# Two staging buffers for the pieces of G, and the final normalization on GpSimd

## What is computed

```python
queries = (query @ Wq + bq).reshape(B, L, H, E)
keys_flat = k @ Wk + bk                      # k: the 32 patterns, the same for every batch
values = (keys_flat @ Wv + bv).reshape(B, S, H, D)
A = sparsemax(einsum('blhe,bshe->bhls', queries, keys) / sqrt(E))
out = einsum('bhls,bshd->blhd', A, values)
x = layernorm(x + transpose(out, (0, 2, 1, 3)).reshape(B, L, H * D) @ Wo + bo)
s = einsum('btd,dm->btm', x, Win) + bin_
g = einsum('btmh,mh->btm', relu(s[..., None] * W1 + b1), W2) + b2
x = layernorm(x + einsum('btm,md->btd', g, Wout) + bout)
```

## Time and profile before

| | before |
|---|---|
| median of 3 runs | 1370.93 us (1370.77 to 1371.69) |
| the profiled execution | 1371.21 us, of which the span from first to last instruction is 1369.4 |
| PE, DVE, ACT, POOL busy | 90%, 84%, 79%, 62% of the span |
| DMA | 333.89 MB, 244 GB/s in the mean |
| the chain that ended last | DMA 4%, PE 4%, ACT, POOL and DVE 1% each |

### The profile page before, as it was taken

One profiled execution on the slowest core, in us unless ns is written; L12 is line 12 of the kernel. 1 busy time (PEld: TensorE's weight loads), 2 busy tenths in 40 slices (PEclk: granted clock), 3 DMA queues, 4 the chain that ended last, 5 costly groups with the idle time before them and its releaser, 6 DMA issues. The chain is left out here.

```text
span 1369.4 us, 25981 instructions
## 1 busy us (share of the span) xinstructions
PE 1238.4 (90%) x6104; PEld 917.0 (67%) x6104; DVE 1155.0 (84%) x4538; ACT 1078.6 (79%) x2317; POOL 851.5 (62%) x1676
## 2 busy tenths in 40 slices
PE   9954557599999999999999999999999999989885
PEld 6632334477777777777777777777777777756552
DVE  4847555798999999999999999999999999957666
ACT  3634254467899999999999999999999999977666
POOL 1532334454567777777777777777777767766654
PEclk9976667899999999999999999999999999999998
DMA  6455355898778788888888888888888888789983
GB/s 202 124 135 146 76 143 147 235 333 254 247 259 268 266 265 263 270 274 270 266 266 266 261 270 273 276 263 268 266 263 265 271 275 265 241 268 345 333 274 100
DMA packets 96793, 333.89 MB, mean 244 GB/s; under 512 B 16580, under 2 KB 16580, under 8 KB 80231
## 3 DMA queue, kind: packets, MB, share of 16 engines
q1 hardware_dynamic: 96470, 331.76, 76.4%
q10 hardware_dynamic: 144, 0.26, 0.1%
HBM read 273.24 MB, written 58.72 MB: 242 GB/s over the span
## 5 line engine op out<-in xcount | busy, mean ns | idle before, releaser
L825 PE MATMUL bank<-G_sb,pT 128*128 128x512 f32 x512 | 244.5, 600 | 11.1 <-DMA G_sb<-G_of_heads 9.9
L1462 DVE MAX8 top<-bank 128x8 f32<-128x32 f32 x2048 | 211.4, 175 | 0.0
L816 PE MATMUL bank<-A_hi,xT_hi 128*128 128x512 f32 x512 | 205.3, 401 | 0.0
L817 PE MATMUL bank<-A_lo,xT_hi 128*128 128x512 f32 x512 | 205.2, 401 | 0.0
L818 PE MATMUL bank<-A_hi,xT_lo 128*128 128x512 f32 x512 | 204.7, 400 | 0.0
L1512 DVE SCALAR_TENSOR_TENSOR acc<-hinge,w2c,acc 128x512 f32<-128x512 f32 x210 | 156.5, 745 | 51.9 <-ACT hinge L1096 51.7
L605 POOL TENSOR_TENSOR rstd<-ve,minus_half 128x1 f32<-128x1 f32 x244 | 172.9, 709 | 43.0 <-POOL ve L600 42.7
L1066 ACT ACTIVATE unread<-y_sb,minus_mean 128x512 bf16<-128x512 f32 x244 | 174.5, 715 | 24.6 <-POOL minus_mean L592 23.6
L1096 ACT ACTIVATE hinge<-s_sb,b1c,w1c 128x512 f32<-128x512 f32 x240 | 192.6, 805 | 0.0
L592 POOL TENSOR_TENSOR minus_mean<-sum,per_row 128x1 f32<-128x1 f32 x244 | 86.1, 359 | 133.9 <-DVE y_sb L1355 133.6
L1355 DVE SCALAR_TENSOR_TENSOR y_sb<-bank,y_sb 128x512 f32<-128x512 f32 x244 | 159.3, 657 | 10.0 <-DMA y_sb<-in_L_attn_query_dram 8.8
(11 more groups left out here) (172 smaller groups left out, 3144.8 us busy)
## 6 DMA issues: line engine op xcount, KB each, us to landing
G_sb<-G_of_heads SPq DMA_DIRECT2D x128, 1536.0 KB, 7.7
x_sb<-in_L_attn_query_dram SPq DMA_DIRECT2D x128, 256.0 KB, 6.5
y_sb<-in_L_attn_query_dram SPq DMA_DIRECT2D x256, 128.0 KB, 7.2
out_dram<-o_sb SPq DMA_DIRECT2D x230, 128.0 KB, 6.5
G_of_heads<-y_sb SPq DMA_DIRECT2D x96, 256.0 KB, 4.1
out_dram<-y_sb SPq DMA_DIRECT2D x11, 256.0 KB, 3.3
y_sb<-in_L_attn_Wk_dram SPq DMA_DIRECT2D x1, 1024.0 KB, 5.7
y_sb<-in_L_attn_Wq_dram SPq DMA_DIRECT2D x1, 1024.0 KB, 7.9
```

The lines of the kernel that those rows point to most:

```text
L816: nc.tensor.matmul(ps[:], hi[:, c, :], w_hi[:, c, :], start=start and c == 0, stop=False)
L817: nc.tensor.matmul(ps[:], hi[:, c, :], w_lo[:, c, :], start=False, stop=False)
L825: nc.tensor.matmul(o[:], p_blocks[:, block_of(i, c), i % HPC, :], G[:, raw_col(c), :].bitcast(F32), start=(c == RAW[0]), stop=False)
L1462: mx = nc.vector.max(top8[:, h, :], z_ps[i % 2][:, h * S:(h + 1) * S])
```

## The change

The three kinds of staged pieces get two buffers each, used in turn by the units of a kind. Raw: y_sb rows 0 to 3 and o_sb. Unrounded copies and rests: y_sb rows 4 to 7 and 8 to 11. Rounded parts: the first four rows of G_sb's buffers 1 and 2, written with their own type. ScalarE's waits ask for the stores up to the last but one of a kind. SP issues raw and rounded stores one slot after their unit, in place of two; the rests stay at three. New waits of SP hold the loads of G for heads 1 and 2 until the staged parts in their buffers have been read and stored; the waits ahead of the first rows of x follow the new places. The row `bout_row` moves from o_sb to the tile `both`.

The final normalization up to slot 130 (95 tiles) moves from ScalarE to GpSimd, right behind the second `norm` of the slot, with its waits for the shift and for the store of four tiles before.

```diff
@@ -191,7 +191,7 @@
         kp_sb, c_full, bv_row = (
             hinge[0:S, 0, :], hinge[0:1, 1, :], s_sb[0:1, 1, :])
         Wout_sb = s_sb[:, 0, :]
-        bout_row = o_sb[0:1, 2, :]
+        bout_row = both[0:1, :]
         rounded = split[0:1, :]
         K_blk = acc[:].rearrange("p (c n) -> p c n", c=C)
         bk_c = sb("bk_c", [P, C])
@@ -388,7 +388,19 @@
 
             return hi_col(c) + 1
 
-        STAGE_RAW, STAGE_LO, STAGE_HI = 0, HPC, 2 * HPC
+
+        def stage_raw(k):
+
+            return (y_sb[:, 0:HPC, :], o_sb[:])[k // (2 * HPC) % 2]
+
+        def stage_lo(k):
+
+            first = HPC * (1 + k // (2 * HPC) % 2)
+            return y_sb[:, first:first + HPC, :]
+
+        def stage_hi(k):
+
+            return G_sb[:, 1 + k // (2 * HPC) % 2, 0:HPC, :]
 
         def turns_of(turn, j, lag, ring):
 
@@ -485,7 +497,7 @@
                 for n in range(HPC):
                     places = G_dram[HPC * heads + n].rearrange("(a s) n -> s a n", s=S)
                     sp.dma_start(places[:, :, col * D:(col + 1) * D],
-                                 y_sb[n * S:(n + 1) * S, stage:stage + HPC, :]).then_inc(s_stored, 16)
+                                 stage[n * S:(n + 1) * S]).then_inc(s_stored, 16)
 
             def slot(turn, j):
                 base = turn * UNROLL
@@ -493,19 +505,19 @@
                 if XR <= n < TILES:
                     sp.wait_ge(s_xT, n - XR + 1)
                     sp.dma_start(x_sb[:, n % XR, :], x_tiles[n // UNROLL, n % UNROLL]).then_inc(s_x[n % XR], 16)
-                for k in pieces(turn, j - 2)[HPC - 1:]:
+                for k in pieces(turn, j - 1)[HPC - 1:]:
                     heads, c, a = piece(k)
                     if in_parts(k):
                         sp.wait_ge(s_Ghi, parts_to(k))
-                        store_unit(heads, hi_col(c), STAGE_HI, s_Gst_hi)
+                        store_unit(heads, hi_col(c), stage_hi(k).bitcast(F32), s_Gst_hi)
                     else:
                         sp.wait_ge(s_Gev, k + 1)
-                        store_unit(heads, raw_col(c), STAGE_RAW, s_Gst_raw)
+                        store_unit(heads, raw_col(c), stage_raw(k), s_Gst_raw)
                 for k in pieces(turn, j - 3)[HPC - 1:]:
                     heads, c, a = piece(k)
                     if in_parts(k):
                         sp.wait_ge(s_Glo, parts_to(k))
-                        store_unit(heads, lo_col(c), STAGE_LO, s_Gst_lo)
+                        store_unit(heads, lo_col(c), stage_lo(k), s_Gst_lo)
                 if in_range(turn, j, LAG_G):
                     i = base + j - LAG_G
                     h = i % H
@@ -515,15 +527,19 @@
                             sp.wait_ge(s_Gst_raw, 16 * HPC * len(RAW) * units)
                             sp.wait_ge(s_Gst_hi, 16 * HPC * len(IN_PARTS) * units)
                             sp.wait_ge(s_Gst_lo, 16 * HPC * len(IN_PARTS) * units)
+                    if i in (1, 2):
+                        sp.wait_ge(s_Glo, PIECES // 2 - (HPC if i == 1 else 0))
+                        sp.wait_ge(s_Gst_hi, 16 * (PIECES // 2 - (HPC if i == 1 else 0)))
                     if i >= GR:
                         sp.wait_ge(s_o, i - GR + 1)
                     sp.dma_start(G_sb[:, i % GR].bitcast(F32).rearrange("p c n -> p (c n)"), G_dram[h]).then_inc(
                         s_G[i % GR], 16)
                 if in_range(turn, j, LAG_XB):
                     i = j - LAG_XB
-                    for row, s_stored in ((STAGE_RAW, s_Gst_raw), (STAGE_LO, s_Gst_lo), (STAGE_HI, s_Gst_hi)):
-                        if base + i == row:
-                            sp.wait_ge(s_stored, 16 * (PIECES // 2))
+                    if base + i == 0:
+                        sp.wait_ge(s_Gst_raw, 16 * (PIECES // 2))
+                    if base + i == HPC:
+                        sp.wait_ge(s_Gst_lo, 16 * (PIECES // 2))
                     halves = [x_rows[turn + i // H, i % H, half] for half in range(2)]
                     if not isinstance(turn, int) or base + i >= YR:
                         sp.wait_ge(s_final, base + i - YR + 1)
@@ -625,6 +641,12 @@
                     i = j - LAG_FINAL
                     norm(base + i + 1, i % 2, s_var2, var2, s_ve2, ve2, s_mean2, minus_mean2, s_rstd2, rstd2,
                          s_shift2, shift2, s_final)
+                    if not vector_finishes(turn, j):
+                        pool.wait_ge(s_shift2, base + i + 1)
+                        if base + i >= OR:
+                            pool.wait_ge(s_store[i % OR], 32 * turns_of(turn, j, LAG_FINAL, OR))
+                        nc.gpsimd.tensor_scalar(o_sb[:, i % OR, :], y_sb[:, i % YR, :], rstd2[:, i % 2:i % 2 + 1],
+                                                shift2[:, i % 2:i % 2 + 1], ALU.mult, ALU.add).then_inc(s_final, 1)
                 if base + j == TILES + LAG_SCORE:
 
                     pool.wait_ge(s_score, TILES)
@@ -681,8 +703,8 @@
                     if in_parts(k):
                         a = k % HPC
                         pool.wait_ge(s_Ghi, parts_to(k))
-                        nc.gpsimd.tensor_tensor(y_sb[:, STAGE_LO + a, :].bitcast(F32R), y_sb[:, STAGE_LO + a, :],
-                                                y_sb[:, STAGE_HI + a, :], ALU.subtract).then_inc(s_Glo, 1)
+                        lo, hi = stage_lo(k)[:, a, :], stage_hi(k)[:, a, :]
+                        nc.gpsimd.tensor_tensor(lo, lo, hi.bitcast(F32), ALU.subtract).then_inc(s_Glo, 1)
 
             slots(pool, slot)
 
@@ -1121,15 +1143,6 @@
                             act.wait_ge(s_var, squares)
                     nc.scalar.activation(by_head(unread[:]), u_of(i), ACT.Sign,
                                          accum_out=count2[:, i % UR:i % UR + 1]).then_inc(s_count2, 1)
-                if in_range(turn, j, LAG_FINAL) and not vector_finishes(turn, j):
-
-                    i = j - LAG_FINAL
-                    act.wait_ge(s_shift2, base + i + 1)
-                    if not isinstance(turn, int) or base + i >= OR:
-                        act.wait_ge(s_store[i % OR], 32 * turns_of(turn, j, LAG_FINAL, OR))
-                    nc.scalar.activation(o_sb[:, i % OR, :], y_sb[:, i % YR, :], ACT.Identity,
-                                         bias=shift2[:, i % 2:i % 2 + 1], scale=rstd2[:, i % 2:i % 2 + 1]
-                                         ).then_inc(s_final, 1)
                 if in_range(turn, j, LAG_Y) and not vector_finishes(turn, j):
                     i = j - LAG_Y
                     act.wait_ge(s_shift1, base + i + 1)
@@ -1187,17 +1200,17 @@
                 for k in pieces(turn, j):
                     heads, c, a = piece(k)
                     act.wait_ge(s_Gmm, k + 1)
-                    stored = 16 * HPC * (k // HPC // 2)
+                    stored = 16 * HPC * (k // HPC // 2 - 1)
                     if in_parts(k):
-                        if a == 0 and k >= 2 * HPC:
+                        if a == 0 and stored > 0:
                             act.wait_ge(s_Gst_hi, stored)
                             act.wait_ge(s_Gst_lo, stored)
-                        nc.scalar.copy(y_sb[:, STAGE_LO + a, :], G_ps[a][:]).then_inc(s_Gev, 1)
-                        nc.scalar.copy(y_sb[:, STAGE_HI + a, :].bitcast(F32R), G_ps[a][:]).then_inc(s_Ghi, 1)
+                        nc.scalar.copy(stage_lo(k)[:, a, :], G_ps[a][:]).then_inc(s_Gev, 1)
+                        nc.scalar.copy(stage_hi(k)[:, a, :], G_ps[a][:]).then_inc(s_Ghi, 1)
                     else:
-                        if a == 0 and k >= 2 * HPC:
+                        if a == 0 and stored > 0:
                             act.wait_ge(s_Gst_raw, stored)
-                        nc.scalar.copy(y_sb[:, STAGE_RAW + a, :], G_ps[a][:]).then_inc(s_Gev, 1)
+                        nc.scalar.copy(stage_raw(k)[:, a, :], G_ps[a][:]).then_inc(s_Gev, 1)
 
             slots(act, slot)
 
```

## The result

The changed kernel takes 1311.2 us (median of 4 runs, 1310.79 to 1314.18) beside 1370.85 of the kernel before; the ratio is 0.957, 95% interval 0.9553 to 0.9586. The forecast was 1310 in 1299 to 1338. The profiled execution is the longest of the four, 1314.18 us with a span of 1312.4; no trace of the other three is there, so where its 3 us lie stays open. What the traces of the 14 kernels of this document show is where such differences can lie: from tile 40 to tile 127 all but e7's took 771.4 us, and from tile 127's line to the end they took 180.9 to 190.8 us, and the edits hardly touch that part (184.4 in before, 184.3 in after). For an edit in the stage the starts of the tiles therefore say more than the totals. Against the profiled execution of before it is 57.0 us shorter.

The account below looks back on a forecast made before the run. The prediction took TensorE to bound the steady stage at 8.87 us a tile and ScalarE's waits for stores the stage making G; -71.5 + 4.4 + 10 - 4.6 = -61.7 from 1371.2 gave 1310 us, range 1299 to 1338.

Parts of the forecast that it names:

- The waits: Stage making G: ScalarE's seven waits for G's stores go with the second staging buffers, -71.5 us.
- (a): Stage making G: unit u+4 waits for unit u's stores, 1.1 us in four short pairs, 4.4 us stay.
- (b): Pair 7 to 9: exact sort partly lay beside ScalarE's wait; 8.5 to 11.8 us come back, taken as 10.
- (c): Stage's three long pairs: TensorE no longer restarts at 1.2 GHz, 0 to 9.3 us gained, taken as 4.6.
- rival 2: TensorE stays at 1.2 GHz in the stage, so every pair takes 18.2 us; 1332 us in total; 12%.
- The sum of the stage: Stage making G: waits removed, smaller wait, lost sort cover and warmer TensorE together give -61.7 us.
- "Nothing" for the loads of G: New waits before G's loads of heads 1 and 2 cost nothing: 13 us against 10.5 for landing.
- Part 2: Final normalization on GpSimd, 95 tiles: no gain as TensorE bounds, no cost as idle time takes the 0.77 us.
- VectorE's hold-up: Steady stage: GpSimd's new step holding up VectorE only replaces another hold-up, 0 us; at most 0.39 us a tile.
- rival 3: VectorE's hold-up comes on top in every tile, 37 us back, 1347 us in total; 10%.
- Room for one more step: Per tile: one more full hold-up of VectorE could cost at most 0.39 us; delays behind GpSimd's both and means cost 0.
- Rivals 1, 4 and 5: Stores drain one group at a time, 1349, 8%; GpSimd's held-up step slows VectorE, 1438, 3%; wait merely moves, about 1370, 2%.

Follow-up runs that it names:

- e7: Changed kernel with GpSimd making each of the 95 final normalizations twice; 1343.0 us, 0.9793 of the kernel before.
- e3: Changed kernel with SP issuing the rests of unit u ahead of the rounded parts of unit u+2; 1308.11 us, 0.9521 of the kernel before.
- e5: Kernel before with the exact sort left out; 1355.58 us, 0.9877 of the kernel before.
- e6: Changed kernel with the exact sort left out; 1285.01 us, 0.937 of the kernel before.
- e12: Changed kernel with two buffers only for unrounded copies and rests, one each for raw pieces and rounded parts; 1338.33 us, 0.9747 of the kernel before.
- e9: Changed kernel with 105 filling matmuls put before TensorE's wait for the sort; 1315.0 us, 0.9577 of the kernel before.
- e4: Changed kernel with G's load for head 0 issued ahead of the eight stores in its slot; 1306.99 us, 0.9509 of the kernel before.
- e10: Changed kernel with both the rests stored first and head 0's G loaded first; 1307.92 us, 0.9529 of the kernel before.
- e1: Changed kernel with the final normalization left on ScalarE, so the staging buffers alone; 1314.59 us, 0.9569 of the kernel before.
- e2: Kernel before with only the final normalization moved to GpSimd, single staging buffers; 1372.09 us, 0.9998 of the kernel before.
- e11: Changed kernel with rests stored first, head 0's G loaded first and 105 filling matmuls during the sort; 1306.3 us, 0.9524 of the kernel before.

## Why the prediction was right, step by step

The mechanism held and the total is 1 us off the median. That it is so near is partly luck: a loss of 4.9 us was put at nothing (below), and single executions of one kernel lie 3 us and more apart. The pairs between parted units' first copies, in us from one start to the next unit's readiness, with the mean granted clock where it isn't 1.00:

```
pair     1-3   3-5        5-7        7-9 (sort)  9-11       11-13      13-15      sum
before  13.0  18.2(.64)  13.1(.64)  34.3(.56)   13.5(.62)  18.2(.64)  13.1(.64)  123.4
after   12.9  15.6(.89)  13.0       43.0(.64)   13.0       17.8(.81)  13.0       128.3
```

- **The waits, -71.5.** Right. They are gone but for 5.3 us, of which 0.5 are waits for a bank, not for stores.
- **(a) A smaller wait stays, +4.4.** Right in size, not in number: I had 1.1 us in each of four short pairs (14.3 against 13.2); it was 1.5 to 1.7 in three (14.5 to 14.7 against 13.0), 4.8 in all. Ahead of unit 3 the code asks for no store at all (`stored` is 0: its buffer is fresh), so the first pair had no term to be counted. The drain was as worked out: eight stores issued from 175.96 on, the last landed 10.4 us after the start of the issues, for 2.6 + 7.9 = 10.5. And e3 shows that it was the order on SP's queue.
- **(b) The sort's cover, +10.** Right: 10.4 by e5 and e6. Counted from the sort's place it is 12.1, a little over the 11.8 of the range. The pair itself grew by 8.7 us: without the sort it takes 18.2 in e5 and 14.6 in e6, so the sort added 16.1 in before and 28.4 in after, 12.3 more, and the pair without it is 3.6 shorter.
- **(c) A warmer TensorE, -4.6.** The middle of an open range, so that it came near is luck: the two long pairs without the sort lost 2.6 and 0.4, and in e6, where the third is free of the sort, it takes 14.6 against 18.2. Over all kernels but e12, which waits elsewhere, the pairs from start to readiness stand so:

```
granted clock            0.92 to 1.00   0.89, 0.90     0.81     0.74   0.60 to 0.65
long pair, us            14.6 to 14.8  15.4 to 16.2  17.7, 17.8  19.4  18.0 to 19.0
short pair, us           12.2 to 13.1        -            -        -   13.1 to 13.7
```

  So the 3.1 us in doubt, 3.6 as measured, come and go with the slow clock. That they are its doing is argued from this order, into which the 19.4 (e9) doesn't fit; no run changed the clock alone. The prediction's rival 2 (every pair 18.2) fell: after has one near it, 17.8.
- **The sum of the stage.** (b) and (c) together were to be +5.4 and are 128.3 - 123.4 = +4.9, in which the short pairs' own -0.8, at nothing in the forecast, is included. Unit 15 starts 133.6 us after unit 1, where 133.1 was worked out.
- **"Nothing" for the loads of G: wrong.** I looked at the new waits ahead of heads 1 and 2 and not at head 0, whose load has no new wait but stands behind eight stores that the faster stage now issues right before it. From tile 21 to 26 61.8 - 56.9 = 4.9 us were lost. With head 0's load ahead of the stores 2.5 of them are lost all the same (e4), so some 2.4 us are this load's place, and what takes the others is open: the transfers that meet there, as argued under e10, weren't moved one by one. The stage itself was 61.8 us ahead at tile 21, where 61.7 was worked out; with this term the sum would have been 1309.5 + 4.9 = 1314.4, and the profiled execution, in which the term was measured, took 1314.2. That the other three executions took 1311 isn't explained, for want of their traces; the closing part alone differs by up to 10 us from trace to trace.
- **Part 2, 0.** Right by e1 and e2. By rows, GpSimd's idle time before the means fell from 1.05 to 0.35 us a tile, 0.70 of the 0.79 that the step takes. Its share rose to 77.55% in the window and not to 82; over 400 to 1100 us it went from 71.9 to 79.0%, 49.7 us for 62.6 of new work, and its powers (L621) and L616 fell by 7.6 and 10.3. In e1, without the moved step, they didn't fall (743 and 286 ns beside 737 and 282 in before, 689 and 217 in after), so that is the step's doing; by which mechanism wasn't tried.
- **VectorE's hold-up, 0.** Right, and better than that: L1446 went from 927 to 692 ns and L1401 from 412 to 358, L1439 from 175 to 280, and VectorE from 95.69 to 94.51 of 100 us. The hold-up exists (0.69 against 1.73 us in the earlier trace rows), but the added step took it from L1446 instead of adding to it: 692 ns as the mean of 79 is hardly held up at all. e1 (926 ns) and e2 (695) show that this is the moved step's doing. That it does it by shifting what GpSimd runs beside L1446 is argued, not shown. So rival 3 fell. The Trainium skill's page "SBUF — State Buffer", section "Who interferes with whom", states the lock on which that rival stood; the trace agrees with the lock, and not with a price for it in every tile.
- **Room for one more step: overrated.** The most I gave to one more full hold-up was 0.39 us a tile, through VectorE. e7 adds 0.78 us to GpSimd and costs 0.30 a tile with GpSimd at 85.67%. The size is under that bound. What I had put at nothing is ScalarE behind GpSimd's "both" and means: for one added step that held (7.6 us of waits), for the second it didn't (54.2 us). How the loss divides between this road and VectorE's hold-up is open.
- **Rivals 1, 4 and 5** have nothing left: no wait of 4 us for a store, 8.87 us a tile afterwards, 57 us gained. The mean granted clock from unit 1's to unit 15's first copy was 0.84 (0.73 in before), over the 0.8 that was to show the forecast right.

e3 (0.9521) and e4 (0.9509) are both faster than after (0.9569) by their middle values, about 0.5%. e4's interval ends just below after's (0.9546 and 0.9553), e3's overlaps it, and its case rests on the waits that are gone from its trace. Between the two the runs don't tell. The kernel to take is e4's, or e3's.

## What to carry to other kernels

Find the bound of each stage by its own waits, remove the wait, and then add back what lay under it: here the sort's 10 us and the smaller wait of 5. Count such a wait only where the code asks for one. When a stage gets faster, look through the queue for every transfer issued at its end, not only for those with a new wait: what used to have time now stands behind the stores. Before a gain of a few us is given to an edit, look whether it is already there ahead of the edit's place, as half of e4's was. And an engine at 78% of its time may have no 0.8 us a tile to give, where its steps sit in a chain through other engines.

## What the runs showed of the hardware

- With TensorE standing through the sort the granted clock was 0.50, and with it busy through the sort 1.00 (after and e11, 110 to 120 us). Where the dips fall moves from kernel to kernel, and a long pair took 14.6 us at 1.00 and 18.2 at 0.64. Of the two kernels with 105 fillers in the sort one came out 3.8 us behind its like (e9 -53.1, after -56.9), the other 2.9 ahead (e11 -64.6, e10 -61.7).
- A 128x128 f32 matmul of one line came as two instructions: 210 fillers gave 420, 47.1 us in all, 0.11 us each.
- The DMAs moved 374 GB/s from 210 to 220 us in e10 (share 1.04), mostly loads of G and of rows: the last four stores of G were issued by 204.2. In the stage of before, with stores and few loads, they moved 266 (60 to 66 us).
- The same GpSimd step took 0.77 us, and 1.27 or 1.28 in three of 95 (after, L648). What held it in those three wasn't looked into.
